# GpSimd forms the last points of an image's first unit, and ScalarE's second high part comes ahead of its first copies

## The reference

```
x = x + attention(group_norm(x))      # layer norm, 1x1 and depthwise 3x3 convolutions to q, k, v,
                                      # attention over channels, 1x1 projection
x = x + conv(group_norm(x))           # 96 -> 96 channels: 1x1, 3x3, 5x5 and dilated 3x3 branches,
                                      # concatenated, then a 1x1 convolution of 384 -> 96 channels
```

## Time and profile before

| | |
|---|---|
| Time, median of 3 runs | 1709.49 us (1707.55 to 1710.29) |
| Profiled execution, first to last instruction | 1706.1 us |
| TensorE busy with matmuls | 1652.5 us, 97% |
| VectorE busy | 1488.7 us, 87% |
| ScalarE busy | 1022.2 us, 60% |
| GpSimd busy | 579.8 us, 34% |
| Mean granted TensorE clock | 0.975 of full speed |

### The profile page before, as it was taken

How to read it: one execution, slowest core, us unless ns; L and a number is a source line. 1 busy time by engine, 2 the same in 40 slices (tenths; PEclk the granted TensorE clock), 3 DMA queues, 4 the chain that set the end, 5 groups by cost and what they waited for, 6 DMA issues and landing times.

```text
span 1706.1 us, 38231 instructions
## 1 busy us (share of the span) xinstructions
PE 1652.5 (97%) x13285; PEld 1552.1 (91%) x13285; DVE 1488.7 (87%) x1964; ACT 1022.2 (60%) x1665; POOL 579.8 (34%) x398
## 2 busy tenths in 40 slices
PE   6999999999999999999999999999999999999998
PEld 6989959999999996999999996899999999599998
DVE  6788879999888859999978886999988887799997
ACT  4856576555385658545546666755446566765551
POOL 4999931222281003232247002123326400312222
PEclk9999979999999997999999999899999999799999
DMA  7012115666502201666630220366661121055553
GB/s 192 0 47 65 38 32 136 177 164 172 153 2 61 69 19 44 157 167 172 169 95 15 69 65 1 87 165 175 167 165 46 35 73 41 1 133 139 135 144 104
DMA packets 105017, 166.01 MB, mean 97 GB/s; under 512 B 40266, under 2 KB 78763, under 8 KB 104780
## 3 DMA queue, kind: packets, MB, share of 16 engines
q1 hardware_dynamic: 81772, 138.95, 32.0%
q10 hardware_dynamic: 23168, 26.04, 4.7%
HBM read 52.20 MB, written 25.17 MB: 45 GB/s over the span
## 4 chain that ended last, share of the span: by engine, by line
PE 84%; DVE 7%; issue 4%; ACT 3%; DMA 1%; DVEq 0%; SPq 0%; POOL 0%; ACTq 0%; POOLq 0%
PE ps L957 41%; PE ps L796 12%; PE ps L817 8%; PE ps L819 7%; PE ps L818 7%; PE ps L845 3%; PE ps L879 3%; PE ps L952 1%; PE ps L752 1%; ACT region L1178 1%; DVE region L1706 1%; DVE region L1676 1%; ACT region L1111 1%; DVE X L1514 1%; DVE region L1673 1%
## 5 line engine op out<-in xcount | busy, mean ns | idle before, releaser
L957 PE MATMUL ps<-region,W 128*96 128x256 f16 (+2 forms) x7140 | 800.7, 270 | 10.0 <-DMA region<-region 5.4
L957 PEld LDWEIGHTS ps<-region,W 128*96 128x96 f16 (+1 forms) x7140 | 771.3, 122 | 31.8 <-issue 14.8
L1428 DVE TENSOR_TENSOR region<-V,band 128x2322 f32<-128x2322 f32 (+2 forms) x104 | 257.8, 2488 | 59.5 <-PE ps L819 56.1
L1178 ACT ACTIVATE region<-region 96x1584 f16<-96x1584 f32 (+2 forms) x80 | 98.4, 1272 | 309.1 <-DVE region L1610 309.1
L701 POOL TENSOR_TENSOR region<-region 96x528 f32<-96x528 f32 (+1 forms) x72 | 92.0, 1282 | 445.9 <-DVE region L1676 328.4
L817 PE MATMUL ps<-region 128*128 (+1 forms) x1152 | 228.1, 280 | 10.4 <-DVE region L1428 4.5
L819 PE MATMUL ps<-region 128*128 (+1 forms) x1152 | 222.8, 275 | 0.0
L818 PE MATMUL ps<-region 128*128 (+1 forms) x1152 | 222.2, 274 | 0.0
L1706 DVE SCALAR_TENSOR_TENSOR region<-ps,small,region 96x768 f32<-96x768 f32 (+1 forms) x220 | 203.7, 988 | 12.1 <-PE ps L957 10.4
L796 PE MATMUL ps<-proj,region 96*128 96x240 f32 x1024 | 209.3, 367 | 0.6 <-DVE region L1402 0.6
L796 PEld LDWEIGHTS ps<-proj,region 96*128 96x128 f32 x1024 | 194.8, 191 | 14.1 <-DVE region L1402 1.0
(11 more groups left out here) (234 smaller groups left out, 2199.8 us busy)
## 6 DMA issues: line engine op xcount, KB each, us to landing
region<-region SPq DMA_DIRECT2D x104, 247.5 KB, 3.9
region<-in_x_dram SPq DMA_DIRECT2D x128, 192.0 KB, 2.3
out_dram<-region SPq DMA_DIRECT2D x40, 576.0 KB, 4.2
region<-region ACTq DMA_DIRECT2D x72, 247.5 KB, 2.4
X<-in_x_dram SPq DMA_DIRECT2D x30, 576.0 KB, 6.2
region<-region SPq DMA_DIRECT2D x32, 247.4 KB, 4.9
X<-in_x_dram SPq DMA_DIRECT2D x19, 384.0 KB, 10.6
region<-region SPq DMA_DIRECT2D x24, 185.6 KB, 3.7
```

The costliest lines, as they stand in the source:

```text
L957: last = mm(o, w, src, start=k == 0, stop=k == len(steps) - 1, skip_group_check=split and ck > 0)
L1178: act.activation(dst[0:C, a:e, x:z], src, ACT.Copy, scale=1.0 if whole else col(SA)).then_inc(s_h, 1)
L1428: v.tensor_tensor(T[:, i, 3 * c:3 * c + m].rearrange("p m (i j) -> p m i j", j=3), taps.broadcast_to([P, m, BW // 3, 3]), mask.broadcast_t ...
```

## The change

In unit 0 of each image, GpSimd gets three more instructions at the end of `first_planes`: it forms planes 0 and 2 of blocks 1 to 4 and their part 1 sums. [...] VectorE forms planes 0 and 2 and the sums of block 0 alone; its two plane steps stand ahead of the first low part, and the sums between the first and the second low part. On ScalarE `plain(hi, 1)` comes ahead of `copied(0, 2)`, so the number of a high part among the eight counted steps changes, and TensorE's and VectorE's waits are set to it: TensorE waits for 5 steps and not for 4 ahead of the first product, VectorE for 3 and not for 5 ahead of the second low part. ScalarE waits for GpSimd's 15th and 16th step.

```diff
-        NFP, NPL0 = 13, 9
+        NFP, NPL0 = 16, 9
...
                     for c in range(2):
                         take(slots(0, 3, c), taps(2, c, 3), taps(0, c, 3))
+                    done(13)
+                    outer = pln[:, 1:5, 0:4 * RW].rearrange("p k (t e) -> p k t e", e=2 * RW)[:, :, :, 0:RW]
+                    pair = lambda x: pln[:, 1:5, x * RW:(x + 2) * RW].rearrange("p k (t e) -> p k t e", e=RW)
+                    less = f32at(Y2F_AT + YF * RW, 8 * RW).rearrange("p (k t e) -> p k t e", k=4, t=2)
+                    take(less, pair(1), pair(0))
+                    done(14)
+                    take(outer, less, pair(0))
+                    done(15)
+                    rows3 = pln[:, 1:5, 0:3 * RW].rearrange("p k (q e) -> p k q e", e=RW)
+                    pool.tensor_tensor(cs[1][:, 1:5].rearrange("p k (q j) -> p k q j", j=PC), rows3[:, :, :, PC:RW],
+                                       rows3[:, :, :, 1:1 + PC], ALU.add).then_inc(s_fp, 1)
...
-                                pe.wait_ge(s_h, n * NH + 4 + START)
+                                pe.wait_ge(s_h, n * NH + 5 + START)
...
                         sums(hi, 0)
+                        act.wait_ge(s_pl0, b * NPL0 + 8 + START)
+                        act.wait_ge(s_fp, b * NFP + 15 + START)
+                        plain(hi, 1)
                         copied(0, 2)
-                        act.wait_ge(s_pl0, b * NPL0 + 8 + START)
-                        plain(hi, 1)
                         act.wait_ge(s_pl0, b * NPL0 + 9 + START)
+                        act.wait_ge(s_fp, b * NFP + 16 + START)
                         sums(hi, 1)
                         midway()
...
                 def second_part():
 
-                    slot = lambda k: pln0[:, :, k * RW:(k + 1) * RW]
                     first_done(6)
-                    dve.wait_ge(s_fp, b * NFP + 13 + START)
-                    v.scalar_tensor_tensor(slot(0), slot(0), -2.0, slot(1), ALU.mult, ALU.add).then_inc(s_pl0, 1)
-                    v.scalar_tensor_tensor(slot(2), slot(1), -2.0, slot(2), ALU.mult, ALU.add).then_inc(s_pl0, 1)
+                    v.scalar_tensor_tensor(plane0(0, 0, 1), plane0(0, 0, 1), -2.0, plane0(0, 1, 2),
+                                           ALU.mult, ALU.add).then_inc(s_pl0, 1)
+                    v.scalar_tensor_tensor(plane0(0, 2, 3), plane0(0, 1, 2), -2.0, plane0(0, 2, 3),
+                                           ALU.mult, ALU.add).then_inc(s_pl0, 1)
+
+                def second_part_sums():
+
                     first_done(8)
-                    pairs = pln0[:, :, 0:3 * RW].rearrange("p k (q e) -> p k q e", e=RW)
-                    v.tensor_tensor(cs0[1].rearrange("p k (q j) -> p k q j", j=PC), pairs[:, :, :, PC:RW],
-                                    pairs[:, :, :, 1:1 + PC], ALU.add).then_inc(s_pl0, 1)
+                    pairs = plane0(0, 0, 3).rearrange("p (q e) -> p q e", e=RW)
+                    v.tensor_tensor(cs0[1][:, 0].rearrange("p (q j) -> p q j", j=PC), pairs[:, :, PC:RW],
+                                    pairs[:, :, 1:1 + PC], ALU.add).then_inc(s_pl0, 1)
...
-                        plain(part, (1, 5)[part])
+                        plain(part, (1, 3 if whole == 0 else 5)[part])
...
                 second_part_edge()
+                second_part()
                 lows(0, 0, 0, 0, 0)
-                second_part()
+                second_part_sums()
                 lows(0, 0, 0, 0, 1)
```

## The result

The changed kernel takes 1714.25 us (median; 1712.85 to 1717.18) and the kernel before, run beside it, 1710.35 (1707.55 to 1712.91). The ratio is 1.0028, with a 95% interval of 1.0021 to 1.0036: slower by 4.8 us (3.6 to 6.2). The two medians alone differ by 3.9 us. The forecast was slower by 9.2 us, to 1718.7. The profiled executions span 1706.1 us before and 1711.2 after, a difference of 5.1 us.

What follows compares the result with a forecast made beforehand. TensorE's convolution products were taken as the bound, idle only 10.0 us. Later starts of 15.8 us less 6.6 us of removed stalls gave +9.2 us on 1709.5, so 1718.7 us; range 1709 to 1722.

Steps and rivals of the forecast that it cites:

- The hold: In the image statistics, GpSimd's new instructions block VectorE's small steps with two SBUF operands, twice an image; chance 0.75.
- The term of the hold: Statistics ahead of unit 0: GpSimd's 7.1 us of new instructions delay each image 3.94 us, four images 15.8 us.
- the pair of rows 6: Image 0: VectorE's step at 210.66, GpSimd's instruction at 210.69; GpSimd wins and the step lasts 1.15 us.
- The term of the stalls: First two units of the four images: TensorE's waits behind unit 0's first product go, gaining 6.6 us.
- All five waits: TensorE's waits in units 0 and 1 behind unit 0's first product, together 6.74 us, all predicted to go.
- First product: Unit 0's first TensorE product was to come 14.4 us after line 1573's start, not 10.4.
- The first unit's steps: Unit 0: VectorE's point steps fit before its low part, ScalarE's 1.27 us wait goes, unit 1 planes start 1.9 us earlier.
- Not held: Rival: VectorE's tiny statistics steps pass and GpSimd gives way; 1702.9 us; chance 0.13.
- One hold only: Rival: only the statistics step of 247.68 is held, 1.85 us an image; 1710.3 us, no change; chance 0.08.
- Gain lost by colliding transfers: Rival: unit 0's second-part transfers land late or slow the first part's; up to 6.6 us lost, 1725.3; chance 0.04.
- The granted clock: Before image 0's first products: a later rise costs half a us per us at the lower level; changes the range only.
- the step of 42.79: VectorE step taking 0.16 us beside a GpSimd instruction from 42.76; evidence for no hold, explained by possible order of issue.

Runs made afterwards that it cites:

- run 1: Kernel before plus three GpSimd instructions of the same shapes as the change's, writing to spare memory nobody reads: 1721.69 us, ratio 1.0077.
- run 2: Kernel before plus four GpSimd memsets of 96 x 1700 in spare memory, which read nothing: 1708.99 us, ratio 1.000.
- run 4: Changed kernel with four statistics steps written as tensor_scalar, one tensor operand and per-partition scalars: 1706.44 us, ratio 0.9989 to the kernel before.
- run 5: Changed kernel without GpSimd's third new instruction; VectorE forms the sums of all 5 blocks: 1708.42 us, ratio 0.9991 to the kernel before.
- run 3: Changed kernel without GpSimd's three new instructions, one memset in their place, part of the computation left out: 1701.33 us, ratio 0.9951 to the kernel before.
- run 7: Changed kernel with third-instruction sums on VectorE, four tensor_scalar statistics steps, block 0 row differences moved behind line 1595: 1701.45 us, ratio 0.9949 to the kernel before.
- run 6: Changed kernel with GpSimd's three new instructions waiting until VectorE has written the norm's scale and offset: 1728.22 us, ratio 1.0114 to the kernel before.

## Why the prediction was right, and where its sizes were off

**Direction and mechanism: right.** The hold was read from two steps of image 0 and carried to another place of the kernel. Run 1 shows it by itself, run 2 that a GpSimd instruction that only writes doesn't do it, run 4 that VectorE's step needs two SBUF tensor operands. The Trainium skill, "SBUF — State Buffer", section "SBUF: two separate sides", says this of two-input VectorE steps and a reading GpSimd instruction; runs 1, 2 and 4 agree with it, by 1.97, 0.15 and 0.21 us for the same step.

**The size: about half.** The time is 4.8 us longer and not 9.2. The loss was put too high by 2.8 us and the gain too low by 1.4, so both errors move the sum the same way. 1714.25 us lies inside the stated range, but well below the forecast of 1718.7.

**The term of the hold: 13.0 us and not 15.8.** Two assumptions fail. The first is the length of GpSimd's third instruction, 1.86 us and not 2.2: its twelve runs of 66 were costed nearly in proportion to four of them, which overstates it by 0.34 us an image. The second is which step the third instruction holds. The step of line 1590 starts 0.03 us ahead of it, like the pair of rows 6, but passes. Line 1591 is held in its place, to the same end, and its own 0.22 us, which the sum put behind the hold, lie inside it. The two make 0.56 of the 0.69 us between the 3.94 forecast and the 3.25 measured for an image; small shifts of starts are the rest. The estimate from "GPSIMD Engine Reference", section "3.1 Elementwise" of the Trainium skill was 6.4 us for the three; 4.92 + 1.86 = 6.8 was measured, between it and the 7.1 of the sum.

**The term of the stalls: 8.0 us and not 6.6.** All five waits went, as predicted. But each image became 2.0 us shorter, where rows 2 list 1.64 to 1.72, and the start times of single products in the traces show why. Products that follow without a wait start 0.11 us apart. In image 0 of the kernel before, unit 1's third point starts 1.97 us after the product ahead of it, so 1.86 us are lost. The idle time before a matmul is reckoned from a modelled end of the one ahead, 0.27 us behind its start, and says 1.70. And unit 0's third point starts 0.24 us after the product ahead of it, 0.13 us late, which shows as no idle time at all. 1.86 + 0.13 = 1.99 us: unit 1's third point comes 29.01 us after the first product before the change, and 27.02 after it. The page's idle column, 10.0 to 4.2 us, would have given 5.8.

**First product: nearly.** It comes 13.68 us after line 1589's start (261.46 - 247.78), where 14.4 was forecast and 10.4 stood before; the error is that of the hold.

**The first unit's steps: right.** The two point steps fit ahead of the low part, ScalarE's wait is gone, and VectorE's unit 1 planes start 9.05 us after the scale step and not 11.03 (1.9 earlier was forecast). The prediction says of the kernel before, too, that these planes wait for the rows for unit 1; there it was VectorE's own low parts that ended last, at 261.71, behind the rows at 261.20. In the changed kernel they do wait for the rows, by 0.76 us. Unit 1's third point comes 27.0 us after the first product in all four images; 27.3 to 27.5 was forecast, from the 1.70 us of the idle column.

**The rivals.** Not held: this falls with run 1. One hold only: this falls, since the changed kernel has two held steps; run 5 makes a kernel with one, and its 1708.42 us against 1709.42 is near the no change that this rival gave. Gain lost by colliding transfers: this falls with the 203.2 to 203.4 us of the convolution in the changed kernel and in runs 3, 5 and 7. The granted clock: it cost the changed kernel nothing. The idle time ahead of the second average grew from 0.52 to 3.81 us in image 0, and the rise to the upper level came at the end of the window of 256 to 258 us, whose mean granted clock is 0.52: still some 3.5 us before the first product. It did cost one stage of run 4: in image 1, where the wait ahead of the first product was 2.15 us, the first 24 products took 4.36 us, and 0.9 us of the gain was lost. The windows of that stretch, columns as in run 6:

```profile
670.00:672.00 2.00, 0.58 (x6) 0.61 (x7) 1.45 (x2) 2.00 (x3) 0.00 (x0) 1.00 0.87 193
672.00:674.00 2.00, 2.00 (x14) 1.93 (x13) 1.26 (x2) 2.00 (x2) 0.00 (x0) 0.62 0.50 102
```

It falls from 1.00 to 0.62 just behind the wait.

**Open.** Why line 1590 passes, starting 0.03 us ahead of GpSimd, while the step of 210.66 is held at the same 0.03 us. There are two candidates, and no run separates them. One is which of the two came first, which starts this close don't settle, least of all on GpSimd, whose spans the profile gives only roughly: a step that starts with a GpSimd instruction, at 203.46 in the kernel before, is held (0.60 for 0.22 us), while one that starts with GpSimd's third in run 6, at 255.84, passes with its 0.28 us, and GpSimd takes 2.02 us and not 1.86. The other is the operands. Line 1590 multiplies a column with itself, and so does the step of 42.79, which passes though it starts 0.03 us behind GpSimd; every held step reads two different columns or stretches of rows. So the step of rows 8, which the prediction counts for "not held" and explains by order, may be a kind of step that isn't held at all. And where the prediction says that the trace agrees with the rule, that is so for the hold; the order in which the two engines get in is not shown.

## What to carry to other kernels

Before work is given to an idle GpSimd, look at what VectorE does in that stretch, not at how busy it is. Here a step with two SBUF operands and one number per partition, 0.16 us long, became as long as the rest of GpSimd's instruction, and on a chain of small steps that is paid in full. Statistics written as tensor_scalar with per-partition scalars passed, for 0.06 us each, but the next two-operand step then paid, so the order has to be laid out for the whole stretch. The rearrangement, which the profile's idle times put at 6.6 us, was worth 8.0. GpSimd's part cost 13.0, and only taking the two apart showed that a version 8 us faster than the kernel before could be had.

## What the runs showed of the hardware that was not expected

- A GpSimd memset of 1.6 us beside VectorE's two-operand steps stretches none of them (run 2).
- GpSimd's instructions get longer too. Its third took 1.94 to 1.95 us in run 4, where it starts inside VectorE's line 1545, and 2.02 in run 6, where it starts with a two-operand step; in run 1 and the changed kernel it took 1.86. In run 6 the first two took 5.41 us for 4.92.
- After 6.95 us without a product TensorE's granted clock was at 0.50, and the next 24 products took 4.57 for 2.83 us (run 6). After a wait of 2.15 us in image 1 of run 4 it fell as well, and they took 4.36.
